# Weighing one attention head in four on GpSimd, four buffers for expert rows, and a new static order in a fused two-layer decoder

## The reference

```
x = LN(x + gated_linear_recurrence(x))
x = LN(x + window_attention(x, ctx))            # first attention, windows of 128
x = LN(x + quantised_lora_ffn(x))
x = LN(x + alibi_attention(x))                  # second attention, 512 x 512
# third attention ("masked"):
attn = softmax(q k^T / 4 + (1 - mask) * -1e9)
attn = attn * group_prob[:, None]               # the same weights for all heads
x = LN(x + (attn @ v) wo + bo)
x = x + latent_causal_attention(rmsnorm(x))     # fourth attention
x = x + top2_of_8_experts(rmsnorm(x))           # 256 -> 512 -> 256, silu
x = LN(x)
```

## Time and profile before

| | |
|---|---|
| time, median of 3 runs | 1552.52 us (1545.74 to 1553.4) |
| the profiled execution: its time | 1553.4 us |
| its span, first to last instruction | 1551.6 us |
| busy: PE, DVE, ACT, POOL | 1421.7, 1068.9, 793.6, 145.0 us |
| third attention, about 690 to 1070 us | 380 us |
| between the two expert batches, 1417 to 1426 us | 9 us |
| behind the last matmul, 1516.2 to 1551.6 us | 35.4 us |

### The profile page before, as it was taken

The page is one execution under the profiler, slowest core; times in us unless marked ns, Lnnn a source line. Parts: engine busy times, 40 slices in busy tenths (PEclk is TensorE's granted clock), DMA queues, the critical chain, the costliest instruction groups (busy, mean ns, idle before and its releaser), DMA issues. The chain is left out here.

```text
span 1551.6 us, 29461 instructions
## 1 busy us (share of the span) xinstructions
PE 1421.7 (92%) x9744; PEld 799.8 (52%) x9744; DVE 1068.9 (69%) x2424; ACT 793.6 (51%) x1512; POOL 145.0 (9%) x166
## 2 busy tenths in 40 slices
PE   6788899999999999999999999999999989898990
PEld 3456576563564445433343343333545545787990
DVE  5786753565564777689999999998768785241415
ACT  5465655536547565555455455555656545332330
POOL 1110120100100001001010000000000021012304
PEclk8899999999999999999999999999999999998995
DMA  7223223501402123133132221111223224965753
GB/s 225 76 72 101 54 74 104 169 8 50 123 32 53 48 79 120 49 91 92 38 99 78 76 83 50 49 47 50 60 53 90 53 84 139 338 225 184 253 183 115
DMA packets 119346, 154.07 MB, mean 99 GB/s; under 512 B 31746, under 2 KB 99714, under 8 KB 117250
## 3 DMA queue, kind: packets, MB, share of 16 engines
q1 hardware_dynamic: 116132, 143.80, 31.1%
q0 software_dynamic: 3072, 8.39, 1.6%
HBM read 73.23 MB, written 18.35 MB: 59 GB/s over the span
## 5 line engine op out<-in xcount | busy, mean ns | idle before, releaser
L1577 ACT ACTIVATE prob<-ps 128x512 f32<-128x512 f32 (+3 forms) x832 | 407.1, 550 | 248.6 <-PE ps L1348 124.1
L1869 DVE TENSOR_REDUCE mx<-ps 128x1 f32<-128x512 f32 (+3 forms) x512 | 281.9, 584 | 89.6 <-PE ps L1315 48.3
L1348 PE MATMUL ps<-of_expert 99*128 99x512 bf16 (+4 forms) x768 | 252.8, 355 | 7.4 <-DMA of_expert<-mrow 6.1
L1348 PEld LDWEIGHTS ps<-of_expert 99*128 99x128 bf16 (+1 forms) x768 | 72.7, 98 | 101.2 <-ACT prob L1577 39.1
L2041 DVE SCALAR_TENSOR_TENSOR room_b<-room_b,ps 128x512 f32<-128x512 f32 x46 | 31.5, 687 | 130.6 <-ACT room_b L1612 113.2
L1385 PE MATMUL ps<-prob,va 128*32 128x512 f32 (+3 forms) x1024 | 115.3, 525 | 0.0
L1313 PE MATMUL ps<-of_expert 102*128 102x512 bf16 x256 | 94.4, 380 | 2.2 <-issue 0.5
L1308 PE MATMUL ps<-of_expert 96*128 96x512 bf16 x256 | 87.6, 384 | 8.1 <-DVE mx L1865 6.9
L1865 DVE CUSTOM_DVE_ANT_0 ps<-ps,room_a 128x512 f32<-128x512 f32 x128 | 86.0, 707 | 4.6 <-PE ps L1308 4.3
L1865 DVE CUSTOM_DVE_ANT_0 ps<-ps,room_b 128x512 f32<-128x512 f32 x128 | 85.8, 708 | 1.1 <-PE ps L1308 0.9
L1305 PE MATMUL ps<-of_expert 96*128 96x128 bf16 (+3 forms) x256 | 71.6, 302 | 9.3 <-DVE mx L1869 7.4
(11 more groups left out here) (219 smaller groups left out, 2620.2 us busy)
## 6 DMA issues: line engine op xcount, KB each, us to landing
of_expert<-parts SPq DMA_DIRECT2D x384, 128.0 KB, 2.4
room_a<-in_w SPq DMA_DIRECT2D x38, 512.0 KB, 5.6
room_b<-in_w SPq DMA_DIRECT2D x18, 512.0 KB, 5.5
otc<-oraw SPq DMA_DIRECT2D x256, 32.0 KB, 2.0
sorted<-y SPq DMA_DIRECT2D x2, 2944.0 KB, 10.4
pack<-sorted SPq DMA_DIRECT2D x46, 128.0 KB
expert_out<-room_b SPq DMA_DIRECT2D x46, 128.0 KB
ct<-in_c SPq DMA_DIRECT2D x8, 512.0 KB, 3.5
```

The source lines that it names most:

```text
L1348: i = pe.matmul(dst[:, lo:S], ks[0:rows, h, t], qs[0:rows, h, lo:S], start=(a != MASKED), stop=(a != CAUSAL and not fixed))
L1577: act.activation(prob[:, quad % PROBS, n, lo:S], key_bank(*st)[:, lo:S], ACT.Exp).then_inc(s_exp, 1)
L1869: i = dve.tensor_reduce(mx[:, slot, s, n:n + 1], src[:, 0:width], AX.X, ALU.max)
```

## The change

Three things are changed together.

1. A new step EG: GpSimd weighs head 0 of each quad (128 x 512), VectorE's first E step weighs head 1 alone (128 x 512) and the second heads 2 and 3 as before. V waits for both.
2. `xin` and `outr` get four buffers in place of two (`ROWS_IN`, `ROWS_OUT`); the new ones lie in `wa`, where the weights of the attentions were. EX, ED and CG wait accordingly. The first layer norm of the first layer (n = 0) gets small buffers of its own (`norm_buffer`), and `stats`, `mv`, `ve`, `rstd`, `shift` grow to four.
3. Nearly all numbers of the table `LAG` are new, and with them the order of the steps in the whole program.

```diff
+ROWS_IN, ROWS_OUT = 4, 4
-    return {0: 0, 2: 0, 5: 0}.get(n, 1)
+    return {0: 3, 2: 0, 5: 0}.get(n, 1)
...
                 if a == MASKED:
                     grouped += [("E", u, g, s, 0), ("E", u, g, s, 1)]
+                    shared += [("EG", u, g, s)]
...
-        return [("DVE", 1.15, [(("T", u, g, s, 2 * h + 1), "ACT")] + more)]
+        return [("DVE", (0.62, 1.2)[h], [(("T", u, g, s, 2 * h + 1), "ACT")] + more)]
+    if kind == "EG":
...
+        return [("POOL", 1.6, [(("T", u, g, s, 0), "ACT"), (("ML", seq_of(u), 2), "SP")] + room)]
...
-LAG = {"IN": -2.9, "EA": -1.2, "CA": 3.7, ("CA", 0): 7.6, ("CA", 1): 16.7, "FS": 7.7, "FZ": 19.8, "SO": 8.5, "OP":
+LAG = {"IN": 20.1, "EG": 7.4, ("EG", 2): -1.4, "EA": -1.0, "CA": -6.1, ("CA", 0): 9.7, ("CA", 1): 7.5, "FS": -3.6,
...
-        outr = [room_b[:, 3584 + i * D:3584 + (i + 1) * D] for i in range(2)]
-        xin = [pack[:, XIN_AT + i * D:XIN_AT + (i + 1) * D] for i in range(2)]
+        outr = [room_b[:, 3584 + i * D:3584 + (i + 1) * D] for i in range(2)] + [wa[:, (2 + i) * D:(3 + i) * D] for i in range(2)]
+        xin = [pack[:, XIN_AT + i * D:XIN_AT + (i + 1) * D] for i in range(2)] + [wa[:, i * D:(i + 1) * D] for i in range(2)]
...
-                    if at > 1:
-                        sp.wait_ge(s_eh, at - 1)
-                    sp.dma_start(xin[at % 2], xs[k][i * P:(i + 1) * P, :]).then_inc(s_ex[at % 2], 16)
+                    if at >= ROWS_IN:
+                        sp.wait_ge(s_eh, at - ROWS_IN + 1)
+                    elif at > 1:
+                        sp.wait_ge(s_qk, nth("QK", UNITS - 1, 0, 0))
+                        sp.wait_ge(s_qk, nth("QK", UNITS - 1, 0, 1))
+                    sp.dma_start(xin[at % ROWS_IN], xs[k][i * P:(i + 1) * P, :]).then_inc(s_ex[at % ROWS_IN], 16)
...
                         pe.wait_ge(s_e, nth("E", u, g, s, 1))
+                        pe.wait_ge(s_eg, nth("EG", u, g, s))
...
-                    if at > 1:
-                        act.wait_ge(s_eo[at % 2], 16 * (at // 2))
-                    act.activation(outr[at % 2], side_bank(*st)[:, 0:D], ACT.Copy).then_inc(s_edc, 1)
+                    if at >= ROWS_OUT:
+                        act.wait_ge(s_eo[at % ROWS_OUT], 16 * (at // ROWS_OUT))
...
+                    act.activation(outr[at % ROWS_OUT], side_bank(*st)[:, 0:D], ACT.Copy).then_inc(s_edc, 1)
...
+                elif kind == "EG":
+                    u, g, s = st[1:]
+                    quad = QUAD_AT["V", u, g, s]
+                    pool.wait_ge(s_ml[seq_of(u) % 2][2], 16 * (seq_of(u) // 2 + 1))
+                    if quad - GROUPED >= QUAD_AT["V", 2 * NB, 0, 0]:
+                        pool.wait_ge(s_pv, COUNT[QUAD_ITEMS[quad - GROUPED]])
+                    else:
+                        pool.wait_ge(s_dn, DOWN[NB - 1, 1])
+                    pool.wait_ge(s_exp, nth("T", u, g, s, 0))
+                    pool.tensor_tensor(weighed[:, quad % GROUPED, 0, :], prob[:, quad % PROBS, 0, :], masks(seq_of(u))[2][:, s, :],
+                                       ALU.mult).then_inc(s_eg, 1)
...
-                    two = slice(2 * h, 2 * h + 2)
-                    dve.tensor_tensor(weighed[:, quad % GROUPED, two, :], prob[:, quad % PROBS, two, :],
-                                      masks(seq_of(u))[2][:, s:s + 1, :].to_broadcast([P, 2, S]), ALU.mult).then_inc(s_e, 1)
+                    some = slice(1, 2) if h == 0 else slice(2, 4)
+                    dve.tensor_tensor(weighed[:, quad % GROUPED, some, :], prob[:, quad % PROBS, some, :],
+                                      masks(seq_of(u))[2][:, s:s + 1, :].to_broadcast([P, 1 + h, S]), ALU.mult).then_inc(s_e, 1)
```

More of the change, by code:

```diff
@@ L170, in streams @@
     context = []
-    mask, loads, outs, routes, rows, experts, weights, sums, quant, ffn, kept, added, normed = ([] for _ in range(13))
+    mask, loads, outs, routes, rows, experts, weights, sums, quant, ffn, kept, added, normed, shared = ([] for _ in range(14))
     quant += [("LP", n, k) for n in range(2) for k in range(4)] + [("QM",), ("QS",)]
@@ L243, in streams @@
     kept += [("EA", e) for e in range(NE)]
-    return [first, kept, added, normed, ops, turned, values, recips, normal, loads, outs, mask, weights, rows, context, before, later, routes, sums, grouped,
+    return [first, shared, kept, added, normed, ops, turned, values, recips, normal, loads, outs, mask, weights, rows, context, before, later, routes, sums, grouped,
             keys, score, quant, ffn, experts]
@@ L467, in parts_of @@
         more += [(("V", 2 * NB + i // 16, i % 16 // NT, i % NT), "PE")] if i >= 0 else []
-        return [("DVE", 1.15, [(("T", u, g, s, 2 * h + 1), "ACT")] + more)]
+        return [("DVE", (0.62, 1.2)[h], [(("T", u, g, s, 2 * h + 1), "ACT")] + more)]
+    if kind == "EG":
+        u, g, s = rest
+        i = G * NT * (u - 2 * NB) + NT * g + s - GROUPED
+        room = [(("V", 2 * NB + i // 16, i % 16 // NT, i % NT), "PE")] if i >= 0 else []
+        return [("POOL", 1.6, [(("T", u, g, s, 0), "ACT"), (("ML", seq_of(u), 2), "SP")] + room)]
     if kind == "V":
@@ L473, in parts_of @@
         if a == MASKED:
-            more += [(("E", u, g, s, 1), "DVE")]
+            more += [(("E", u, g, s, 1), "DVE"), (("EG", u, g, s), "POOL")]
         if s == 0 and (u, g) != (0, 0):
@@ L547, in parts_of @@
         k = batch_of(b)
-        done = [(("ED", k, TILES[k] - 1), "SP"), (("ED", k, TILES[k] - 2), "SP")]
+        done = [(("ED", k, TILES[k] - 1 - i), "SP") for i in range(ROWS_OUT)]
         i = NT * BATCHES[k].index(b) + t
@@ L785, in decoder @@
         sq = sb("sq", [P, D], BF16)
-        stats = sb("stats", [P, 3, NT, 6])
-        mv = sb("mv", [P, 3, NT, 2])
-        ve = sb("ve", [P, 3, NT])
-        rstd = sb("rstd", [P, 3, NT])
-        shift = sb("shift", [P, 2, NT])
+        stats = sb("stats", [P, 4, NT, 6])
+        mv = sb("mv", [P, 4, NT, 2])
+        ve = sb("ve", [P, 4, NT])
+        rstd = sb("rstd", [P, 4, NT])
+        shift = sb("shift", [P, 4, NT])
         half = sb("half", [P, NT])
@@ L905, in decoder @@
         s_sx = [sem(f"batch_{k}_sorted") for k in range(len(BATCHES))]
-        s_ex = [sem(f"sorted_tokens_{i}_loaded") for i in range(2)]
-        s_eo = [sem(f"expert_out_{i}_stored") for i in range(2)]
+        s_ex = [sem(f"sorted_tokens_{i}_loaded") for i in range(ROWS_IN)]
+        s_eo = [sem(f"expert_out_{i}_stored") for i in range(ROWS_OUT)]
         s_cg = [sem(f"expert_out_{i}_gathered") for i in range(GATHERS)]
@@ L970, in decoder @@
         s_e = sem("weighed")
+        s_eg = sem("first_head_weighed")
         s_pv = sem("values_summed")
@@ L1420, in _ @@
                     at, dst = tile_at(k, i), side_bank(*st)
-                    pe.wait_ge(s_ex[at % 2], 16 * (at // 2 + 1))
+                    pe.wait_ge(s_ex[at % ROWS_IN], 16 * (at // ROWS_IN + 1))
                     for c in range(NC):
-                        i_ = pe.transpose(dst[:, c * P:(c + 1) * P], xin[at % 2][:, c * P:(c + 1) * P], identf)
+                        i_ = pe.transpose(dst[:, c * P:(c + 1) * P], xin[at % ROWS_IN][:, c * P:(c + 1) * P], identf)
                     i_.then_inc(s_eh, 1)
@@ L1615, in _ @@
                     act.wait_ge(s_ed, at + 1)
-                    if at > 1:
-                        act.wait_ge(s_eo[at % 2], 16 * (at // 2))
-                    act.activation(outr[at % 2], side_bank(*st)[:, 0:D], ACT.Copy).then_inc(s_edc, 1)
+                    if at >= ROWS_OUT:
+                        act.wait_ge(s_eo[at % ROWS_OUT], 16 * (at // ROWS_OUT))
+                    elif at > 1:
+                        act.wait_ge(s_qk, nth("QK", UNITS - 1, 1, 0))
+                        act.wait_ge(s_qk, nth("QK", UNITS - 1, 1, 1))
+                    act.activation(outr[at % ROWS_OUT], side_bank(*st)[:, 0:D], ACT.Copy).then_inc(s_edc, 1)
         @block.gpsimd
@@ L1670, in _ @@
                     k = batch_of(b)
-                    for i in range(2):
-                        pool.wait_ge(s_eo[i], 16 * ((sum(TILES[:k + 1]) + 1 - i) // 2))
+                    for i in range(ROWS_OUT):
+                        pool.wait_ge(s_eo[i], 16 * ((sum(TILES[:k + 1]) + ROWS_OUT - 1 - i) // ROWS_OUT))
                     if st == ("CG", BATCHES[0][0], 0):
```

8 lines of the change are left out of this document (4 added, 4 removed), and 27 rows, old and new, of the table LAG.

## The result

The changed kernel is slower: 1565.71 us (median of 4 runs, 1563.85 to 1569.81) against 1549.91 us (median of 4, 1545.74 to 1553.4), ratio 1.0112, 95% interval 1.0094 to 1.0131. I had forecast 1532 us. The profiled execution took 1563.85 us, its span 1562.0 us, at a mean granted clock of 0.97 as before.

What follows compares the result with a forecast made beforehand. VectorE was taken as the third attention's tighter engine by 27 us, PE close behind. Stage 17, border 3.3 and tail 0.9 us, summed as 21 us off 1553.4 us, gave 1532 us, range 1513 to 1562 us.

Steps and rivals of the forecast that it cites:

- The rest of the order: Moved steps outside the third attention and border: no deciding step named, taken as 0, with 10 us either way.
- Rival D: New order loses elsewhere: GpSimd's XB and LS behind waiting EGs, norms late; 10 us lost, 1542 us, chance 0.13.
- The stage: Third attention: shrinks from 380 to 363 us, 17 us less; ends 32 us less and 25 us more.
- VectorE's relief: Third attention: 64 shorter E steps take 33.6 us off VectorE, 367.5 to 333.9 us.
- rival B: Third attention: PE was the bound all along, stage stays within 2 us, border gives 4; 1548 us, chance 0.14.
- The signs that I had named: Third attention if right: VectorE busy near 347 us, short E median 0.69, first to last E about 361 us.
- What GpSimd costs VectorE: Third attention: each EG holds VectorE 0.2 us, 12 to 13 us in sum; ends 0 to 58 us.
- Rival A: Third attention: EG and E start together, VectorE loses nearly the whole hold each time; 1565 us, chance 0.20.
- The border: Between expert batches: four output buffers free ScalarE's copies, PE begins 3.3 us earlier; ends 0 and 4.
- The tail: End of the kernel: GpSimd's gather no longer behind a first-batch norm step, 0.9 us less; ends 0 and 1.

Runs made afterwards that it cites:

- e2: Changed kernel without EG, VectorE weighing all four heads in two equal E steps, new order and four buffers kept; ratio 1.0148 to the kernel before.
- e6: Kernel before with its old order, no EG, only four buffers each for rows in and out and the first norm's own; ratio 0.9997 to before.
- e13: Changed kernel with seven steps (QM, QS, first half of QZ, factor loads) at their old places, warm-ups placed anew; ratio 1.0056 to the kernel before.
- e14: First 62 steps of the old list, then the changed kernel's steps, with EG and four buffers; ratio 1.0091 to the kernel before.
- e3: Changed kernel with head 0's weighing done by neither GpSimd nor VectorE; ratio 1.0007 to the kernel before.
- e1: Kernel before with its old order and two buffers, only EG added and the first E shrunk to one head; ratio 0.9969 to the kernel before.
- e8: Kernel before with its old order, EG and four buffers added, all of the change but the new table; ratio 0.9964 to the kernel before.
- e4: Changed kernel with a GpSimd memset of the same 128 x 512 tile in place of head 0's product; ratio 1.0 to the kernel before.

## Why the prediction was wrong

Forecast and measurement are 38 us apart (21 us faster, 17 slower by the ratio). 23 of them are the order, 12 the third attention, 3 the border.

**The rest of the order: 0, 10 either way.** This is the step that failed. e2 shows the new order and the buffers losing 23 us, and e6 gives the buffers none of it. I wrote that I could name no step whose move decides, and took that for a reason to write 0; the first 200 us did show 39 us of idle PE, which an order can spend as well as save. One candidate could have been named: the difference of the two orders shows the maxima (QM) and the rounding on VectorE behind the first unit's work, and the trace of before had 31.80 us of VectorE's busy time from 20 to 60 us, some 17 of them QM and QZ (4.5, and twice 6). By e13 and e14 it is 3 to 9 us of the 23. Rival D had the right sign with 10 us and the wrong place (behind waiting EGs in the third attention).

**The stage: 380 to 363.** Wrong too, by the size of two terms, and both errors go the same way. The new order has to be kept apart here: it lengthened the stage by 5.7 us (before to e2), so EG is judged from e2 on. VectorE's relief of 33.6 us is right in busy time (e2 to e3: 368.77 to 336.85 us from first to last E, 31.9 less), but worth only 22 us of the kernel's time, where the forecast's 33.6 / 0.967 less 4 us for waits came to 31. In e3 VectorE is idle for 27.6 us and PE waits only 5.3 us for its maxima. So rival B was partly true: PE took over 9 us sooner than I had it. In the old order it was true nearly in full: in e1 VectorE was idle for 31.0 us and the stage 1.8 us shorter, beside 241 warm-ups that I had called no work. The signs that I had named came out accordingly: VectorE 356 us and not 347, the stage 377.4 and not 361.

**What GpSimd costs VectorE: 0.2 us for each EG.** Measured in time, 16 us / 64 = 0.25 us (e3 to the changed kernel), near it, and this is in part luck, since the way I had worked it out was wrong. EG lasts 1.28 us undisturbed, not 1.0, so half of a 128 x 1024 addition was too little, and with its waits its medians are 1.64 and 1.77 us. And RZ and N, which I named only as "a few others", lose too: 0.35 us for each of 8 RZ and 0.49 us for each of 8 N, together 6.7 us, and 2.2 us in the 16 short steps on the maxima, beside 6.2 us in the long E and 3.6 in the short (their means less those of e3, 1272 and 685 ns). That is 18.7 us. From first to last E VectorE's busy time went from 336.85 us in e3 to 356.18 in the changed kernel, 19.3 us. Relief of 22 less 16 leaves the 0.3 to 0.36% of e1, e8 (against e6) and e2 (against the changed kernel), where I expected 17 us.

**Rival A, the lock decides.** Its point, a mean loss of 0.52 us for each EG, wasn't reached (19.3 / 64 = 0.30 us of busy time), and the short E's mean is 0.74 us, not the 1.2 I had set as its sign. The time came out where A had put it, 1565 us, for another reason. One number that fits is no proof of the mechanism: without e1 and e2 A would have looked confirmed.

The Trainium skill's rule (SBUF — State Buffer, Who interferes with whom) that a VectorE instruction with two SBUF inputs and a GpSimd instruction that reads SBUF exclude each other holds here for RZ and N as for E, by the rows above, and the maxima with one input in PSUM show nothing of it (706 and 707 ns for 708 and 707). e4 adds what no row of before could: a GpSimd instruction that only writes didn't hold VectorE (its long products took 1273 ns beside 64 memsets and 1272 without them).

**The border: 3.3 us.** Measured: 0 (e6). ScalarE's wait went as forecast; what I missed is what is late next, the weights, which SyncE issued at 1418.66, behind the loads and the store that had waited for the scatter. **The tail: 0.9 us.** Too small to be told apart, not tested by itself.

What stays open: of the 17 to 19 us that the order costs ahead of the third attention, 8 to 16 have a place (ahead of the third attention) but no named step, the named 3 to 9 have no wait that shows them, the clock's part is unknown, and the 4 to 6 us from the third attention on have no step either.

## What to carry to other kernels

When a change brings a new order with it, price the order by itself first. Look in the opening, where engines have idle time, for long instructions that went from an idle stretch into a busy one: that can be had from the order's difference and one window of the trace, and gives a first candidate to test, here a part of the loss and not the whole. To find where an order loses, splice finished lists of steps; mixed planner tables and the times at which stages begin both pointed at the wrong place. Work given to GpSimd pays what it frees less the holds of every VectorE instruction with two SBUF inputs, not of the relieved one alone, and no more than the next full engine lets through (in e1 VectorE was relieved of 20 us, and the kernel gained 5).

## What the runs showed of the hardware

GpSimd's product of 128 x 512 in fp32 took 1.28 us undisturbed, against 1.99 us for its 128 x 1024 addition: more than half. A GpSimd memset of the same tile took 0.52 us and cost VectorE nothing that e3 to e4 could show. When VectorE's two-input products were under way first, it was GpSimd that waited (2.25 us at 809.60), so that a hold's price isn't one-sided.
